# Reordering the layer steps of a six-layer kernel: projections first in a step, scores last, other PSUM banks

## The chip, the cores and the metric

The kernel runs on one core of one Trainium2 chip. The metric is the device time of one execution in microseconds (us). Below, PE is TensorE (matrix products), DVE is VectorE, ACT is ScalarE, POOL is GpSimd, and SP is the engine that issues most of the DMAs.

## The reference

The input x is 2048 tokens of 128 features. It is normalised to xn, and the result is the sum of three terms:

```
x = L0_attn_x                                   # 1 x 2048 x 128
xn = layernorm(x)
out = x + attention(xn) + layers(xn)

attention: 16 heads of 8, full softmax over 2048 keys, projections of rank 32
layers, 6 times:
  x = attn_layer(shift_tokens(x), Wqkv[i], q_scale[i], k_scale[i], Wo[i]) + x
  x = ffn_layer(shift_tokens(x), ln_g[i], ln_b[i], W1[i], b1[i], W2[i], b2[i]) + x

attn_layer: qkv = x @ Wqkv (128 x 3072); 16 heads of 64; q and k are divided by
  their norms, scaled, rotated; windows of 32 queries see their own and the
  previous window's keys; softmax; @ Wo (1024 x 128)
ffn_layer: layer norm, @ W1 (128 x 682), a * gelu(gate), @ W2 (341 x 128)
```

All is in float32. The kernel cuts the large products into two parts per operand (three products each) where it wants speed at float32 accuracy.

## The kernel before, in words

The program has two parts. Part A (until 780 us of the span) computes the full attention; the change does not touch it. Part B computes the six layers and adds the three terms.

Part B is a software pipeline that is written out by hand. The 2048 tokens of a layer are 16 tiles of 128, and 4 chunks of 512. Over six layers there are 96 tiles (END) and 24 chunks. Each of the five engines walks the same loop, `for u in range(FIRST, LAST)`, and in its step u calls its stages in a fixed order, each for the tile u minus an offset. Engines run in order, so a stage that waits holds up all that stand behind it on its engine. `tile(x)` is x if there is such a tile, `chunk(x)` is a chunk for one x in four (x = 4c + 3), `early(x)` is x for the first 4 steps, and `late(x)` is a chunk of the last layer.

The stages of a tile, in order of the data: `high_x` (ACT) and `low_x` (POOL) cut the input; `project` (PE, q, k, v, six products each); `squares` (ACT), `square_sums` and `root_argument` (DVE), `root_estimate` (ACT, three small operations), `root_slope` and `root_fix` (POOL): the norms; `rotate_cos`, `rotate_sin` (DVE, they read q or k in PSUM), `rotated`, `normalise` (POOL); `turn` (PE, transposes of q and k), `turned_q`, `turned_k` (ACT); `score` (PE, 128 small products), `maxima` (DVE), `exponentials` (ACT, 16 instructions), `prob_sums`, `prob_reciprocals` (DVE), `scale_probs` (POOL), `blocks` (DVE, a transpose within blocks), `move_probs` (SP, eight DMAs); `values` (PE, 128 small products), `values_out` (ACT), `output` (PE), `residual_1` (DVE). The stages of a chunk: `mean`, `deviation`, `deviation_squares`, `variance`, `add_epsilon`, `ln_root_estimate`, `first_scale`, `ln_root_slope`, `ln_root_fix`, `high_ln`, `scale_shift`, `low_ln`, `up_product` (three groups, 0, 2, 1), `gelu` (ACT, between two table loads), `gated` (DVE), `down_product`, `residual_2`.

Let v be the tile whose projection PE does in a step. Then v modulo 4 tells what else PE does in it: 0 variance and down product, 1 nothing, 2 the up products, 3 the mean.

PSUM has eight banks. The dictionary `BANKS` gives each stage its banks for even and odd units, `bank_users` walks PE's order, and `wait_free` makes a stage wait until the last user of each of its banks was read out.

The first four steps also finish part A's result ("dense" stages): `load_dense` (SP), `dense_norm` (DVE, a reciprocal and a product), `dense_output` on PE (L1396) and on ACT (L846), `store_dense` (SP). The last steps add up the result: `final_sum`, `finish`, `final_add`, `store_out`.

Of the kernel before, what the change touches and what calls it, by code (L numbers as in the profile page):

```python
# [16 lines left out]
NT = T // P  # L17
# [11 lines left out]
DEPTH = 6  # L29
# [37 lines left out]
FIRST, LAST = 0, END + 17  # L67
# [45 lines left out]
def late(x):  # L113
# [6 lines left out]
         "q_turn0": ((4,), (4,)), "q_turn1": ((1,), (5,)), "k_turn0": ((6,), (6,)),  # L120
         "k_turn1": ((0,), (7,)), "values": ((6, 7), (6, 7)), "output": ((7,), (7,)),
         "score": ((0, 1), (0, 1)), "mean": ((7,), (7,)), "var": ((4,), (4,)),
         "up0": ((4, 5), (4, 5)), "up1": ((2, 3), (2, 3)), "up2": ((6, 7), (6, 7)),
         "down": ((6,), (6,)), "att": ((7,), (5,)), "finish": ((7,), (7,))}
# [6 lines left out]
def bank_users():  # L131
# [9 lines left out]
    for u in range(FIRST, LAST):  # L141
        take("score", tile(u - 3))
        take("finish", late(u - 12))
        take("q", tile(u - 1))
        take("values", tile(u - 5))
        take("k", tile(u - 1))
        take("output", tile(u - 5))
        take("k_turn0", tile(u - 2))
        take("q_turn0", tile(u - 2))
        take("q_turn1", tile(u - 2))  # L150
        take("mean", chunk(u - 5))
        take("k_turn1", tile(u - 2))
        take("v", tile(u - 1))
        take("up0", chunk(u - 8))
        take("up2", chunk(u - 8))
        take("var", chunk(u - 6))
        take("down", chunk(u - 10))
        take("att", early(u))
        take("up1", chunk(u - 8))
# [250 lines left out]
def sync_b(e, w, m, s, d, out_rows):  # L410
# [93 lines left out]
    for x in range(min(0, -1), END + 12):  # L504
        if 0 < x < END:
            load_rot(x)
        n, i = divmod(x - 0, NT)
        if 0 < n < DEPTH and i == 0:
            load_qkv(n, 0)
        if tile(x - 3) is not None:  # L510
            shift_v(x - 3)
        if early(x - -1) is not None:
            load_dense(x - -1)
# [10 lines left out]
        if c is not None:  # L524
            store_out(c)
        n, i = divmod(x - 0, NT)
        if 0 < n < DEPTH and i == 0:
            load_qkv(n, 1)
        n, i = divmod(x - 7, NT)
        if 0 < n < DEPTH and i == 0:  # L530
            load_w1(n)
# [6 lines left out]
        if early(x - 0) is not None:  # L538
            store_dense(x - 0)
        if tile(x - 3) is not None:  # L540
            move_probs(x - 3)
        n, i = divmod(x, NT)
# [43 lines left out]
def gpsimd_b(e, w, m, s):  # L586
# [66 lines left out]
    for u in range(FIRST, LAST):  # L653
        low_x(tile(u))
        scale_probs(tile(u - 3))
        rotary(tile(u))
        rotated(tile(u - 1), 1)
        root_slope(tile(u - 1))
        root_fix(tile(u - 1))
        normalise(tile(u - 1), 1)  # L660
        normalise(tile(u - 1), 0)
        rotated(tile(u), 0)
# [39 lines left out]
def scalar_b(e, w, m, s):  # L702
# [147 lines left out]
    for u in range(FIRST, LAST):  # L850
# [638 lines left out]
```

## Time and profile before

| | |
|---|---|
| median of 3 runs | 2413.96 us |
| lowest, highest | 2406.57, 2416.26 us |
| profiled execution, its own time | 2408.15 us |
| its span in the profile | 2406.4 us |
| PE busy, share of the span | 90% |
| DVE busy | 83% |
| ACT busy | 73% |
| POOL busy | 54% |

The profiled execution is the source of every duration here. The profile's times count from the start of its span. "Busy" of PE is a modelled figure, since its products overlap.

### The profile page before, as it was taken

What the parts mean: (1) busy time and instruction counts of PE and PEld (TensorE: products, weight loads), DVE (VectorE), ACT (ScalarE), POOL (GpSimd) and SP (SyncE); (2) the same over time, 40 slices, a digit from 0 to 9 for tenths busy, and PEclk for the clock granted to TensorE, in tenths of its full rate; (3) what the DMA queues carried; (4) which work ended last, traced back from release to release, by engine and by line L of the source; (5) the groups of instructions that cost most, each with busy time, mean ns of one, the idle gap of its engine ahead of it and who ended that gap; (6) DMA issues with size and microseconds to landing.
All of it is one profiled execution on the core that took longest, in us unless ns stands there. A gap on an engine that the chain in (4) does not pass through costs nothing. (4 is left out here: it accounts for less than half of the span.)

```text
span 2406.4 us, 82195 instructions
## 1 busy us (share of the span) xinstructions
PE 2162.4 (90%) x34487; PEld 1324.6 (55%) x34487; DVE 2003.7 (83%) x2417; ACT 1758.8 (73%) x4192; POOL 1304.7 (54%) x1085
## 2 busy tenths in 40 slices
PE   5899999999998478989999999999998999999986
PEld 3122222222221267777777777777776777777764
DVE  6899999989992578878888888888988889898863
ACT  1187878878787267877888887788887778788762
POOL 4111111111000378877787887778887778787740
PEclk8599999999999789999999999999999999999987
DMA  1222322232201223343334333433334333433331
GB/s 35 72 75 68 88 55 82 63 83 54 52 22 67 83 68 85 80 123 86 91 82 129 89 89 82 117 101 94 84 84 115 89 92 86 123 92 97 87 80 40
DMA packets 167463, 197.60 MB, mean 82 GB/s; under 512 B 87479, under 2 KB 105141, under 8 KB 167093
## 3 DMA queue, kind: packets, MB, share of 16 engines
q1 hardware_dynamic: 166740, 192.14, 30.6%
q8 instruction: 271, 4.44, 0.8%
q14 instruction: 100, 0.81, 0.1%
q10 hardware_dynamic: 352, 0.20, 0.1%
HBM read 57.83 MB, written 27.26 MB: 35 GB/s over the span
## 5 line engine op out<-in xcount | busy, mean ns | idle before, releaser
L699 ACT ACTIVATE PT<-E_ps 128x512 f32<-128x512 f32 x1024 | 534.4, 601 | 182.3 <-PE E_ps L1242 180.6
L938 DVE TENSOR_REDUCE mx<-S_ps 128x1 f32<-128x1024 f32 x512 | 600.8, 1217 | 27.4 <-PE S_ps L1233 21.6
L639 POOL TENSOR_TENSOR tc<-tc,ts 128x1024 f32<-128x1024 f32 x192 | 462.5, 2409 | 53.8 <-DVE ts L1012 53.4
L647 POOL TENSOR_TENSOR tc<-tc,rs 128x1024 f32<-128x1024 f32 x192 | 362.3, 1909 | 13.8
L1233 PE MATMUL S_ps<-KS,QS 48*128 48x512 bf16 x1024 | 324.9, 401 | 30.4 <-DVE mx L938 22.0
L581 POOL CAST w_cut_b<-w_raw_b 128x512 fp32r<-128x512 f32 (+1 forms) x48 | 27.6, 576 | 550.4 <-DMA w_raw_b<-in_Wqkv 409.8
L762 ACT ACTIVATE pr<-B_ps,mxB 128x64 f32<-128x64 f32 x1536 | 325.0, 372 | 0.0
L1242 PE MATMUL E_ps<-QS,KS 64*128 64x512 bf16 x1024 | 316.2, 385 | 4.7 <-ACT PT L699 4.6
L601 POOL TENSOR_TENSOR pr<-pr,mxB 128x1024 f32<-128x1024 f32 x96 | 184.0, 1916 | 193.5 <-DVE mxB L1045 193.5
L1000 DVE TENSOR_TENSOR tc<-B_ps,rt 128x1024 f32<-128x1024 f32 x192 | 234.8, 1223 | 49.9 <-ACT nrm L710 44.4
L1250 PE MATMUL O_ps<-PT,va 128*32 128x512 f32 x2048 | 276.0, 611 | 0.0
L1274 PE MATMUL B_ps<-w_qkv,x_cut 128*128 128x512 f32 x576 | 262.8, 456 | 10.5 <-ACT q_T L732 6.4
L1242 PEld LDWEIGHTS E_ps<-QS,KS 64*128 64x128 bf16 x1024 | 78.5, 94 | 317.5 <-ACT PT L699 236.3
L710 ACT ACTIVATE nrm<-B_ps 128x1024 f32<-128x1024 f32 x192 | 208.4, 1085 | 61.2 <-PE B_ps L1276 59.0
L1275 PE MATMUL B_ps<-w_qkv,x_cut 128*128 128x512 f32 x576 | 233.5, 405 | 1.9 <-issue 1.9
L1276 PE MATMUL B_ps<-w_qkv,x_cut 128*128 128x512 f32 x576 | 233.3, 405 | 2.1 <-issue 2.1
L982 DVE TENSOR_REDUCE ss<-nrm 128x16 f32<-128x1024 f32 x192 | 232.0, 1208 | 0.0
L1337 PE MATMUL B_ps<-xy,vs 64*64 64x32 f32 x6144 | 204.2, 222 | 23.9 <-issue 16.2
L1337 PE MATMUL B_ps<-xy,v 64*64 64x32 f32 x6144 | 204.4, 222 | 21.3 <-issue 20.8
L1337 PEld LDWEIGHTS B_ps<-xy,vs 64*64 64x64 f32 x6144 | 181.4, 137 | 61.4 <-issue 60.7
L752 ACT ACTIVATE o_T<-B_ps 128x1024 f32<-128x1024 f32 x96 | 98.7, 1028 | 156.7 <-PE B_ps L1337 156.7
L1300 PE MATMUL B_ps<-ident,tc 128*128 128x128 f32 x1536 | 198.6, 276 | 15.6 <-DVE ts L1012 8.9
(191 smaller groups left out, 4139.8 us busy)
## 6 DMA issues: line engine op xcount, KB each, us to landing
xy<-pc SPq DMA_DIRECT2D x768, 64.0 KB, 2.4
vs<-v SPq DMA_DIRECT2D x96, 384.0 KB, 3.7
Wqkv_cut<-w_cut_b SPq DMA_DIRECT2D x72, 256.0 KB, 2.4
w_qkv<-Wqkv_cut SPq DMA_DIRECT2D x36, 512.0 KB, 7.3
rot<-in_rot SPq DMA_DIRECT2D x96, 128.0 KB, 2.7
vs<-v SPq DMA_DIRECT2D x96, 128.0 KB, 3.7
w_raw_b<-in_Wqkv SPq DMA_DIRECT2D x36, 256.0 KB, 3.1
W_cut<-w_cut_b SPq DMA_DIRECT2D x24, 170.5 KB, 2.5
```

The source lines that it names most:

```text
L639: e.tensor_tensor(tc[:, :], tc[:, :], m.ts[i][:, :], ALU.add).then_inc(s[f"rot{n}"], 1)
L647: e.tensor_tensor(tc, tc, m.rs[u % 2][2][:, i * H:(i + 1) * H].unsqueeze(2).to_broadcast([P, H, DH]), ALU.mult).then_inc(s[f"{n}_scaled"], 1)
L699: e.activation(m.PT[n % NPT][:, :], turns.bank("probs", n)[:, :], ACT.Exp).then_inc(turns.sem("probs", n), 1)
L762: a = e.activation(pb[:, :, h, :], sc[:, h, :, :], ACT.Exp, bias=m.mxB[:, 0, h:h + 1], scale=1.0)
L938: e.tensor_reduce(m.mx[h % 2][:, i, hf:hf + 1], m.S_ps[n % 2][:, :, :], AX.XY, ALU.max).then_inc(s["sc_max"], 1)
L1000: e.tensor_tensor(view(m.tcs[u % 2][i][:, :]), raw, wide(m.rt[u % 2][:, 2 * i, :], DH), ALU.mult).then_inc(s[f"rot{n}_c"], 1)
L1233: mm = e.matmul(m.S_ps[n % 2][:, c, :], m.QS[sl][rows, i * P:(i + 1) * P], m.KS[sl][rows, k:k + CH], start=True, stop=True)
L1242: e.matmul(turns.bank("probs", n)[:, :], m.KS[sl][rows, j * P:(j + 1) * P], m.QS[sl][rows, chunk_cols(c)], start=True, stop=True).then_inc ...
L1250: e.matmul(m.O_ps[VC * c:VC * (c + 1), :], m.va[:, j, h, :], m.PT[n % NPT][:, :], start=(j == 0), stop=(j == NT - 1)).then_inc(s["pv"], 1)
L1274: e.matmul(bank, left[0], right[0], start=True, stop=False)
L1275: e.matmul(bank, left[0], right[1], start=False, stop=False)
L1337: mm = e.matmul(bank[at, a, j, b, :], v[r, d:d + DH], m.xy[u % 2][r, b, par * NP + j, :], start=(b == j == 0), stop=True, skip_group_check ...
```

## The change

Each engine's order of stages within a step is changed, and with it the offsets, so that a step starts with `project` and ends with `score`. LAST is END + 16 in place of END + 17. `BANKS` changes for five stages. SP's order changes in four places. No instruction is added or removed, and no size changes.

```diff
-FIRST, LAST = 0, END + 17
+FIRST, LAST = 0, END + 16
...
-         "q_turn0": ((4,), (4,)), "q_turn1": ((1,), (5,)), "k_turn0": ((6,), (6,)),
+         "q_turn0": ((4,), (4,)), "q_turn1": ((6,), (5,)), "k_turn0": ((1,), (6,)),
...
-         "score": ((0, 1), (0, 1)), "mean": ((7,), (7,)), "var": ((4,), (4,)),
+         "score": ((0, 1), (0, 1)), "mean": ((6,), (6,)), "var": ((4,), (4,)),
...
-         "down": ((6,), (6,)), "att": ((7,), (5,)), "finish": ((7,), (7,))}
+         "down": ((5,), (5,)), "att": ((4,), (7,)), "finish": ((7,), (7,))}
```

PE, in tensor_b (bank_users has the same order):

```diff
-        score(tile(u - 3))
-        finish(late(u - 12))
-        project(tile(u - 1), 0)
-        values(tile(u - 5))
-        project(tile(u - 1), 1)
-        output(tile(u - 5))
-        turn(tile(u - 2), 1, 0)
-        turn(tile(u - 2), 0, 0)
-        turn(tile(u - 2), 0, 1)
-        mean(chunk(u - 5))
-        turn(tile(u - 2), 1, 1)
-        project(tile(u - 1), 2)
-        up_product(chunk(u - 8), 0)
-        up_product(chunk(u - 8), 2)
-        variance(chunk(u - 6))
-        down_product(chunk(u - 10))
-        dense_output(early(u))
-        up_product(chunk(u - 8), 1)
+        finish(late(u - 11))
+        project(tile(u), 0)
+        values(tile(u - 4))
+        project(tile(u), 1)
+        output(tile(u - 4))
+        turn(tile(u - 1), 0, 0)
+        turn(tile(u - 1), 0, 1)
+        turn(tile(u - 1), 1, 0)
+        turn(tile(u - 1), 1, 1)
+        project(tile(u), 2)
+        up_product(chunk(u - 7), 0)
+        up_product(chunk(u - 7), 2)
+        up_product(chunk(u - 7), 1)
+        variance(chunk(u - 5))
+        dense_output(early(u))
+        mean(chunk(u - 4))
+        down_product(chunk(u - 9))
+        score(tile(u - 1))
```

DVE, in vector_b:

```diff
-        gated(chunk(u - 9), 2)
-        final_sum(late(u - 11))
-        ln_root_slope(chunk(u - 7))
-        maxima(tile(u - 3))
-        rotate_cos(tile(u - 1), 0)
-        square_sums(tile(u - 1), 0)
-        rotate_sin(tile(u - 1), 0)
-        ln_root_fix(chunk(u - 7))
-        residual_1(tile(u - 5))
-        prob_sums(tile(u - 3))
-        low_ln(chunk(u - 8))
-        rotate_cos(tile(u - 1), 1)
-        prob_reciprocals(tile(u - 3))
-        rotate_sin(tile(u - 1), 1)
-        dense_norm(early(u))
-        final_add(late(u - 11))
-        square_sums(tile(u - 1), 1)
-        root_argument(tile(u - 1))
-        gated(chunk(u - 8), 0)
-        gated(chunk(u - 8), 1)
-        deviation(chunk(u - 5))
-        add_epsilon(chunk(u - 6))
-        blocks(tile(u - 3))
-        residual_2(chunk(u - 10))
-        first_scale(chunk(u - 6))
+        low_ln(chunk(u - 7))
+        first_scale(chunk(u - 6))
+        maxima(tile(u - 2))
+        rotate_cos(tile(u), 0)
+        ln_root_fix(chunk(u - 6))
+        rotate_sin(tile(u), 0)
+        square_sums(tile(u), 0)
+        residual_1(tile(u - 4))
+        prob_sums(tile(u - 2))
+        dense_norm(early(u))
+        prob_reciprocals(tile(u - 2))
+        rotate_cos(tile(u), 1)
+        rotate_sin(tile(u), 1)
+        add_epsilon(chunk(u - 5))
+        final_add(late(u - 10))
+        square_sums(tile(u), 1)
+        deviation(chunk(u - 4))
+        gated(chunk(u - 7), 0)
+        gated(chunk(u - 7), 1)
+        residual_2(chunk(u - 9))
+        blocks(tile(u - 2))
+        final_sum(late(u - 9))
+        root_argument(tile(u))
+        gated(chunk(u - 7), 2)
+        ln_root_slope(chunk(u - 5))
```

ACT, in scalar_b:

```diff
+        scale_shift(chunk(u - 9))
+        root_estimate(tile(u - 3))
+        squares(tile(u - 2), 0)
+        values_out(tile(u - 6))
         exponentials(tile(u - 4))
+        turned_q(tile(u - 3), 0)
         squares(tile(u - 2), 1)
-        turned_q(tile(u - 3), 0)
         turned_q(tile(u - 3), 1)
+        dense_output(early(u - 2))
+        turned_k(tile(u - 3), 1)
         turned_k(tile(u - 3), 0)
-        turned_k(tile(u - 3), 1)
         keep_v(tile(u - 2))
-        deviation_squares(chunk(u - 6))
-        high_ln(chunk(u - 8))
         ln_root_estimate(chunk(u - 7))
-        dense_output(early(u - 1))
         gelu_table(chunk(u - 9))
         gelu(chunk(u - 9), 0)
-        high_x(tile(u))
+        high_ln(chunk(u - 8))
         gelu(chunk(u - 9), 1)
         gelu(chunk(u - 9), 2)
         root_table(chunk(u - 9))
-        scale_shift(chunk(u - 8))
-        root_estimate(tile(u - 2))
-        squares(tile(u - 1), 0)
-        values_out(tile(u - 5))
+        high_x(tile(u))
+        deviation_squares(chunk(u - 6))
```

POOL, in gpsimd_b:

```diff
-        low_x(tile(u))
-        scale_probs(tile(u - 3))
-        rotary(tile(u))
-        rotated(tile(u - 1), 1)
-        root_slope(tile(u - 1))
-        root_fix(tile(u - 1))
-        normalise(tile(u - 1), 1)
-        normalise(tile(u - 1), 0)
-        rotated(tile(u), 0)
+        rotated(tile(u - 2), 1)
+        rotary(tile(u - 1))
+        root_slope(tile(u - 2))
+        root_fix(tile(u - 2))
+        normalise(tile(u - 2), 0)
+        normalise(tile(u - 2), 1)
+        rotated(tile(u - 1), 0)
+        low_x(tile(u))
+        scale_probs(tile(u - 3))
```

SP, in sync_b:

```diff
         if 0 < x < END:
             load_rot(x)
-        n, i = divmod(x - 0, NT)
-        if 0 < n < DEPTH and i == 0:
-            load_qkv(n, 0)
         if tile(x - 3) is not None:
             shift_v(x - 3)
-        if early(x - -1) is not None:
-            load_dense(x - -1)
...
+        n, i = divmod(x - 7, NT)
+        if 0 < n < DEPTH and i == 0:
+            load_w1(n)
         n, i = divmod(x - 0, NT)
         if 0 < n < DEPTH and i == 0:
             load_qkv(n, 1)
-        n, i = divmod(x - 7, NT)
-        if 0 < n < DEPTH and i == 0:
-            load_w1(n)
...
-        if early(x - 0) is not None:
-            store_dense(x - 0)
+        if early(x - 1) is not None:
+            store_dense(x - 1)
         if tile(x - 3) is not None:
             move_probs(x - 3)
+        if early(x - -1) is not None:
+            load_dense(x - -1)
+        n, i = divmod(x - -1, NT)
+        if 0 < n < DEPTH and i == 0:
+            load_qkv(n, 0)
```

## Rows read from the trace of the kernel before

**Rows 1.** Busy time by window: us, then PE, PEld, DVE, ACT, POOL, PEclk, DMA.

```profile
780.00:869.00 89.00, 43.22 (x519) 29.75 (x520) 54.16 (x54) 32.63 (x84) 40.88 (x37) 0.73 0.26 73
869.00:2363.00 1494.00, 1389.46 (x29591) 1100.10 (x29592) 1260.34 (x1652) 1168.89 (x3052) 1152.23 (x926) 0.98 0.37 94
```

**Rows 2.** PE's waits from 780 us on: us in total, times, longest.

```profile
PE B_ps L1337 <- issue: 37.1, 39, 3.3
PE B_ps L1396 <- DVE hid L1153: 27.1, 2, 23.6
PE B_ps L1320 <- issue: 14.9, 8, 5.2
PE B_ps L1315 <- ACT k_T L744: 9.3, 23, 0.4
PE B_ps L1274 <- ACT q_T L732: 6.4, 21, 0.3
PE B_ps L1274 <- DMA w_qkv<-Wqkv_cut: 1.6, 2, 1.0
```

**Rows 3.** Timeline of PE, first steps of part B: start, us, instruction, idle before.

```profile
799.36 2.08 PE L1396 MATMUL B_ps<-hid,w_out 128*128 128x512 f32 x2 [23.62 <-DVE hid L1153]
...
818.10 0.76 PE L1274 MATMUL B_ps<-w_qkv,x_cut 128*128 128x512 f32 x1 [0.87 <-ACT xl L846]
...
834.07 1.06 PE L1315 MATMUL B_ps<-mask_bf,ident_bf 128*128 128x512 bf16 x2
...
836.53 0.50 PE L1274 MATMUL B_ps<-w_qkv,x_cut 128*128 128x512 f32 x1
...
868.74 0.50 PE L1274 MATMUL B_ps<-w_qkv,x_cut 128*128 128x512 f32 x1
```

**Rows 4.** Timelines of POOL, DVE and ACT in the same stretch.

```profile
781.31 0.46 POOL L594 TENSOR_TENSOR x_cut<-stream,x_cut 128x128 fp32r<-128x128 f32 x1
795.23 3.35 DVE L1151 RECIPROCAL hid<-hid 128x512 f32<-128x512 f32 x1 [12.15 <-DMA hid<-l_scratch]
798.62 0.69 DVE L1153 TENSOR_TENSOR hid<-hid 128x512 f32<-128x512 f32 x1
801.48 0.69 ACT L846 ACTIVATE hid<-B_ps,bo 128x512 f32<-128x512 f32 x1 [20.53 <-PE B_ps L1396]
```

**Rows 5.** Timelines of ACT and PE, a step with v = 1 modulo 4.

```profile
1519.15 1.03 ACT L752 ACTIVATE o_T<-B_ps 128x1024 f32<-128x1024 f32 x1 [2.69 <-PE B_ps L1337]
1523.22 1.15 ACT L710 ACTIVATE nrm<-B_ps 128x1024 f32<-128x1024 f32 x1
1526.98 0.59 PE L1315 MATMUL B_ps<-mask_bf,ident_bf 128*128 128x512 bf16 x2 [0.40 <-ACT k_T L744]
```

**Rows 6.** Timelines of DVE and PE, end of a step with v = 2 modulo 4.

```profile
2048.05 0.28 DVE L990 TENSOR_SCALAR rs<-ss 128x32 f32<-128x32 f32 x1
2050.27 1.23 DVE L1023 STREAM_TRANSPOSE pc<-pr 128x1024 f32<-128x1024 f32 x1
2051.43 0.70 DVE L1111 SCALAR_TENSOR_TENSOR hid<-B_ps,b,gel 85x512 f32<-85x512 f32 x1
2052.28 0.32 PE L1337 MATMUL B_ps<-xy,vs 64*64 64x32 f32 x8
```

**Rows 7.** Timelines of DVE and PE, end of a step with v = 0 modulo 4.

```profile
1509.67 1.21 DVE L982 TENSOR_REDUCE ss<-nrm 128x16 f32<-128x1024 f32 x1
1511.15 0.68 DVE L1073 TENSOR_SCALAR lnv<-B_ps 128x512 f32<-128x512 f32 x1
1513.63 0.76 DVE L1125 SCALAR_TENSOR_TENSOR stream<-B_ps,cols,stream 64x512 f32<-64x512 f32 x1
1508.71 2.74 PE L1388 MATMUL B_ps<-hid,w 128*128 128x512 f32 x6
1513.22 0.50 PE L1274 MATMUL B_ps<-w_qkv,x_cut 128*128 128x512 f32 x1
```

**Rows 8.** Timeline of PE in the last steps.

```profile
2355.81 0.50 PE L1274 MATMUL B_ps<-xl_cut,w 128*128 128x512 f32 x1 [1.41 <-DVE xl_cut L1103]
```

More of the change, by code:

```diff
@@ L141, in bank_users @@
     for u in range(FIRST, LAST):
[L142 to L157, printed above, removed]
+        take("finish", late(u - 11))
+        take("q", tile(u))
+        take("values", tile(u - 4))
+        take("k", tile(u))
+        take("output", tile(u - 4))
+        take("q_turn0", tile(u - 1))
+        take("q_turn1", tile(u - 1))
+        take("k_turn0", tile(u - 1))
+        take("k_turn1", tile(u - 1))
+        take("v", tile(u))
+        take("up0", chunk(u - 7))
+        take("up2", chunk(u - 7))
+        take("up1", chunk(u - 7))
+        take("var", chunk(u - 5))
         take("att", early(u))
-        take("up1", chunk(u - 8))
+        take("mean", chunk(u - 4))
+        take("down", chunk(u - 9))
+        take("score", tile(u - 1))
     return users
```

## The prediction

> **What bounds the kernel now.** I read the busy times by window first. From 869 to 2363 us PE is busy for 1389 of 1494 us, at a mean granted clock of 0.98 of full speed; DVE has 84% and ACT 78%. In the 89 us ahead of that, PE is busy for under half, and the clock is 0.73 [rows 1]. So the steady part of part B is bound by PE with some waits, and its start by something else. Then I read PE's waits [rows 2]. "Issue" (PE waits for nothing the profile shows) inside the two runs of 128 small products, values and scores, is 52.0 us: 37.1 + 14.9. Waits for ACT (k_T, q_T) are 15.7 us, in steps with v = 1 and 3 modulo 4. One wait of 23.6 us stands alone: PE's first instruction of part B is the dense product, and it waits for DVE. Last come the timelines of those places.
>
> **The offsets.** Each engine's order is a circle, and what counts is which stages follow each other and for which tile. PE before, in step u = v + 1: scores of tile v - 2, project v, values v - 4, turns v - 1, up v - 7, down v - 9. After, in step u = v: the same tiles, with scores of v - 1 at the end, which is scores of v - 2 ahead of the next. So in the steady state PE's circle is the old one but for small swaps: turns q, q, k, k; the mean behind the v projection; the third up group is already next to the others, as variance and down fall into other steps. ACT's and POOL's circles are also the old ones with neighbours swapped. "One stage less" is therefore no shorter pipeline for a tile; only the dense stages, tied to early(u), move against the rest. The total of the work is the same, and I look for places where a swap touches the path.
>
> **Start of part B (the large term).** Before, PE's step 0 holds only the dense product. It needs a load, then 3.35 and 0.69 us of DVE, and starts at 799.36 [rows 3, 4]. The first projection, whose cut input was ready at 781.31 + 0.46 = 781.8 [rows 4], stands behind it, and the second tile's starts at 818.10 [rows 3]. After, the first tile is projected at 781.8 and the dense product comes behind it. Its data decide as before: I keep 799.4, + 2.08, + 0.69 on ACT (q of the second tile now shares its bank 4) = 802.2 for the second tile's q. That is 818.1 - 802.2 = 15.9 us earlier. Next step, from 802.2: six products at 1.2 GHz, 2.6 (512 columns, 0.43 each); squares 1.1; cosine 1.2 (as the sums), sine in two halves of 0.6, sums 1.2; the dense reciprocal and product 4.0, the dense product on PE 2.1 and its read-out 0.7, which now stands ahead of turned_k on ACT, 1.5; scores 2.5 (834.07 to 836.53). With 0.1 for hand-overs the sum is 18.2, so the third tile's q starts at 820.4, against 836.53 before: 16.1 earlier [rows 3 to 5, 7]. Two steps follow. Before they took 868.74 - 836.53 = 32.2 us, since the last dense product was done early in them [rows 3]. After, both hold one; with a warm PE and the exponentials (3.1 us, 1520.2 to 1523.2 [rows 5]) beside the same list I get 17.0 + 16.7 = 33.7. Bounds: 32.2 as before, and 2 x 18.4 = 36.8 as the step 818.1 to 836.5. The steady state starts 14.6 us earlier (bounds 16.1 and 11.5; at the cheap end nothing is lost again, at the dear end both steps are full ones). The cover of this: nothing in the steady state can give it back, as the whole pipeline starts earlier and PE is its bound.
>
> **Steps with v = 1 and 3 (neutral).** After the values product ACT reads it out (1519.15), does 16 exponentials, then squares of k (1523.22), two q and four k read-outs, and the scores start at 1526.98, having waited 0.40 [rows 5]. The change swaps squares with the first q read-out and the two k's; the list until the last k is the same. The q that the v projection waited for comes 0.95 us earlier, so those 6.4 us of waits go, and the scores' wait for k_T grows by as much: the scores' start is late next, and it is unmoved. The mean behind v instead of ahead of it changes nothing in the sum of PE work ahead of the scores. Gain 0; bounds -6.4 (if ACT's chain had slack) and +2 (24 steps of v = 1 with 0.1 of a swap).
>
> **Steps with v = 2 (a small loss).** The banks 6 and 7 that up group 2 used are the values product's next, so values waits for gated 2. The row shows gated 2 from 2051.43 to 2052.13 and values 0.15 us behind it, at 2052.28 [rows 6]; in all 22 such steps that I read, values starts 0.14 to 0.16 us behind the end of gated 2. This is the path. On it stand gelu 1, gated 1, blocks and gated 2. The change puts root_argument between blocks and gated 2; it occupies DVE for 0.18 us (the 0.28 at 2048.05 overlaps its successor [rows 6]). 23 steps x 0.18 = +4.1 us. Gated 1 can't be earlier, since it waits for the last up product, so the removal of root_argument (and of low_ln, 0.7) ahead of it gives nothing. Bounds 0 and +6.4 (0.28 each).
>
> **Steps with v = 0 (neutral, tight).** The down product moves from bank 6 to 5. Its reader residual_2 now holds up the next q projection (banks 4, 5), 1.6 us sooner than the values product it held up before. Down ends at 1508.71 + 2.74 = 1511.45. DVE, done with the sine at 1509.67, has epsilon 0.60 and sums 1.13 (each less than its row by what overlaps), so it is free at 1511.40, then residual_2, 1.48 for its two halves: 1512.97, + 0.14 = 1513.1. The projection starts at 1513.22 [rows 7]. Slack 0.1: no cost. Bounds 0 and 24 x 0.3 = +7. Blocks and root_argument come 1.5 us behind their old place there; root_estimate then ends about 2 us into the next step, and POOL's fix and two scalings (4.7 us) end at 6.9, where the q turns start and the k turns are 0.9 later. Q is scaled first now, so this holds too.
>
> **SP.** The weights of the next layer's q are issued ahead of load_rot, not behind. One issue is 0.6 us, and the projection waited for that load for 1.6 us in all [rows 2]: -1.6. Load_rot is later by 1.2 to 2 us once a layer; rotary, also one place later on POOL, covers it. The eight moves behind blocks start up to 1.5 us later in one step of four; the values product that needs them is over a step away.
>
> **End.** The last-but-one up product waited 1.41 us for low_ln, which stood behind residual_1 [rows 8]. Now it stands at the head of the step: -1.4. The last chunk's chain is the same.
>
> Sum: -14.6 + 4.1 - 1.6 - 1.4 = -13.5 us. The profiled execution took 2408.15 us (span 2406.4 and 1.75 around it), so 2394.7 for the same execution. The median of the runs shown is 2413.96, 5.8 above it, and I put the difference on the median: 2400.5 us.
>
> The Trainium skill, "Runtime: NRT & Kernel Launch", section "Instruction fetch mechanics", says that an engine fetches its instructions in blocks of 256 while it executes, and that this is hidden. The 52 us of issue in dense runs [rows 2] do not agree if they are fetches. By the page they would be no fetches and the new order would leave them alone, which is my sum; if they are fetches, it may move them, which bears on the first rival's chance.
>
> **Rivals.** (1) Slower: the moves. The eight DMAs behind blocks start 1.5 us later in the 24 steps with v = 0, and so lie wholly over the next values run, the place of most issue waits. For it: those waits are of no engine, so something outside, such as DMA traffic, makes them. Against it: they overlapped that run in part already, and the waits also stand in other steps. Mean of one wait is 37.1 / 39 = 0.95, longest 3.3 [rows 2]; I take 1.5 with what it does to the clock: 24 x 1.5 = +36, so 2436. It decides the sign from 0.56 us a step. (2) The start gains little: rt, loads or the read-out that now stands ahead of turned_k stretch each of the first steps by 2 to 3 us, so that 5 of 14.6 us are left: 2410. For it: DVE is in every one of these steps with 4 us of dense work. Against it: each link was there before. (3) More: bundled waits ahead of the scores give the issue side time, and a third to a half of the 52 us goes: -20, so 2380. For it: the scores' wait becomes one of about 0.9 us just ahead of a dense run. Against it: steps that had such a wait have issue waits as well.
>
> **How the numbers follow.** Forecast 0.55 (its own range 2394 to 2408); rival 1 0.12; rival 2 0.18; rival 3 0.15. About 0.5% (12.1 us) is what a measurement of this kernel can tell from no change. Faster than 2401.9: 0.38 of the forecast, 0.15, and 0.02 of rival 2: 0.55. Within: 0.17 + 0.16 + 0.02 = 0.35. Slower: 0.10. The range reaches from near rival 3 to between rivals 2 and 1: 2383 to 2418.
>
> **What would show it.** Right: PE's first projection at 782; second tile's q at about 802, fifth's at 854 (868.74 before); values still 0.15 us behind gated 2, with L990 between it and blocks; waits for q_T gone and those for k_T doubled; issue waits within a few us of 52. Wrong: a fifth projection after 860 (rival 2), issue waits over 75 us or under 35 us (rivals 1, 3), or q projections that wait for residual_2 (DVE stream, L1125).

## The result, and the profile after

The changed kernel takes 2425.07 us (median; 2417.14 to 2440.6), the kernel before 2414.29 beside it: a ratio of 1.0052 [1.0036, 1.0068] (95% interval), or 12.5 us slower (10.8 between the medians). Once more on another chip it was 1.0036 [1.0013, 1.0059]. The forecast was 2400.5 us and faster; it was wrong in sign, and the range ended at 2418, below both medians (2425.07 and 2420.8).

The profiled execution has a span of 2422.3 us (own time 2424.12) against 2406.4. Busy time by window, the columns as in [rows 1]; the second window goes from the first values product of part B to the last:

```profile
780.00:869.00 89.00, 50.93 (x532) 32.58 (x535) 56.70 (x54) 38.28 (x93) 41.49 (x36) 0.79 0.27 75
872.00:2377.00 1505.00, 1382.23 (x29556) 1097.78 (x29555) 1271.91 (x1650) 1166.65 (x3052) 1151.58 (x922) 0.98 0.36 94
```

PE does the same work at the same clock in 1505 us that took it 1492: the time is idle time. PE's waits from 780 us on show which, answering [rows 2]:

```profile
PE B_ps L1320 <- issue: 35.1, 21, 4.1
PE B_ps L1337 <- issue: 32.4, 41, 3.6
PE B_ps L1315 <- ACT k_T L744: 24.6, 25, 2.3
PE B_ps L1396 <- DVE hid L1153: 14.1, 2, 11.3
```

The waits for q_T are gone, those for k_T have grown (between 869 and 2378 us from 9.3 to 20.0), the wait for w_qkv is gone (1.6 before; 0.2 in a second profile of the changed kernel). What is new is "issue" inside the scores (L1320): 8 waits and 14.9 us have become 21 and 35.1. In values and scores together, the 52.0 us of the prediction have become 67.5. Over all lines of the steady part (from the first values product to the last) the issue waits are 53 with 57.4 us before and 69 with 74.7 us after.

The start, PE's timeline with the answers to [rows 3]: dense product, projections of q for tiles 0 to 4:

```profile
793.07 0.77 PE L1274 MATMUL B_ps<-w_qkv,x_cut 128*128 128x512 f32 x1 [6.12 <-ACT x_cut L782]
...
810.62 2.07 PE L1396 MATMUL B_ps<-hid,w_out 128*128 128x512 f32 x2 [11.31 <-DVE hid L1153]
813.56 0.76 PE L1274 MATMUL B_ps<-w_qkv,x_cut 128*128 128x512 f32 x1 [0.87 <-ACT hid L846]
...
828.84 0.59 PE L1315 MATMUL B_ps<-mask_bf,ident_bf 128*128 128x512 bf16 x2 [2.31 <-ACT k_T L744]
830.78 0.50 PE L1274 MATMUL B_ps<-w_qkv,x_cut 128*128 128x512 f32 x1
...
851.03 0.80 PE L1274 MATMUL B_ps<-w_qkv,x_cut 128*128 128x512 f32 x1
...
869.64 0.79 PE L1274 MATMUL B_ps<-w_qkv,x_cut 128*128 128x512 f32 x1
```

Part A, whose code is the same in both, ends where ACT cuts the first tile (L782): at 791.84 here, at 780.63 before. I count from there, since the end of part A lies anywhere between 774.7 and 791.8 in the profiles of this study. The second tile's q stood 37.5 us behind it and now stands 21.7, as forecast; the fifth's 88.1 and 77.8.

Split of four executions, from the timelines (us; "start" is from the end of part A to the first values product, "values" from the first to the last of the 96):

| | end of part A | start | values | rest | span |
|---|---|---|---|---|---|
| before | 780.6 | 89.7 | 1492.2 | 43.8 | 2406.4 |
| changed | 791.8 | 80.5 | 1504.7 | 45.3 | 2422.3 |
| changed, again (e8) | 785.1 | 81.5 | 1504.7 | 45.3 | 2416.6 |
| best (e14) | 783.1 | 69.5 | 1463.9 | 43.7 | 2360.2 |

So the change gains 8 to 9 us at the start and loses 12.5 us in the steady part, the same in two executions, and 1.5 at the end.

What an issue wait is can be read at one of the longest, in the scores of a step with v = 3 modulo 4. PE's timeline:

```profile
1049.88 1.07 PE L1300 MATMUL B_ps<-ident,tc 128*128 128x128 f32 x8 [0.22 <-ACT pr L762]
...
1053.16 0.60 PE L1315 MATMUL B_ps<-mask_bf,ident_bf 128*128 128x512 bf16 x2
1053.70 1.37 PE L1320 MATMUL B_ps<-k_T,q_T 64*32 64x64 f32 x115
1059.21 0.34 PE L1320 MATMUL B_ps<-k_T,q_T 64*32 64x64 f32 x13 [4.15 <-issue]
```

PE stands with 13 of 128 products to go, and nothing it needs is late. The DMA view of the window 1056.70 to 1056.95 has a row (packets, MB, share) that the windows around it, 1050 to 1056.7 and 1056.95 to 1059.2, do not have:

```profile
q8 instruction: 1, 0.02, 26.9%
```

That queue brings PE's instructions: 271 fetches of 16 KB in an execution, for 69,596 recorded instructions of PE, so 257 to a fetch. The steady part has 234 of them. This one began at 1056.85, and ended 1.3 us before the products went on. The same holds for all 53 waits before and all 69 after, and for 739 of 747 issue waits in fifteen profiles of this study: the last fetch began 2.2 to 3.0 us before the wait's end and ended 1.2 to 1.75 us before it. (In e3, the sixteenth, about a third of 87 waits have no such fetch.) The scores are about 260 instructions in 1.9 us and values 256 in 2.0 us (a matmul comes with its weight load), so a run of them is shorter than the 2.2 us from a fetch's start to the wait's end. If a fetch starts only inside or just ahead of such a run, PE can run out of instructions.

Before and after have almost the same PE stream (69,505 and 69,596 recorded instructions), with the same dense runs. What differs is the waits. A matmul (in the trace, its weight load) carries one wait itself; each further wait goes into separate instructions ahead of it. There are 529 such before and 620 after, so the change does add instructions, 91 waits on PE, though it adds no work: 48 more because k_turn0 of an even tile now lies in bank 1, where the previous scores were, and so waits for the exponentials (smexp) besides k_scaled; 23 ahead of the mean, 21 ahead of projections, and one less elsewhere. In the profile after, fetches start while PE is in the turns 0 times instead of 6, and in the scores 17 times instead of 8, in steps with v = 3.

Theory L: a separate wait that is not yet satisfied holds PE's sequencer, which otherwise runs ahead of PE and asks for the next instructions early. Rivals: R (the new orders on ACT and DVE are late on the path), B (the banks: who waits for whom), N (the number of instructions and where the blocks fall).

### The profile page after: what moved, and what is told of

Same layout as the page of the kernel before. It is cut to its first block and busy times, and to the rows that moved or that the text cites. A ratio compares the mean times of both kernels' runs of the same rounds, so it can differ in the third digit from the quotient of the medians.

```text
span 2422.3 us, 82286 instructions
## 1 busy us (share of the span) xinstructions
PE 2171.9 (90%) x34487; PEld 1328.2 (55%) x34487; DVE 2018.9 (83%) x2417; ACT 1756.9 (73%) x4192; POOL 1306.8 (54%) x1085
## 5 line engine op out<-in xcount | busy, mean ns | idle before, releaser
L938 DVE TENSOR_REDUCE mx<-S_ps 128x1 f32<-128x1024 f32 x512 | 601.3, 1217 | 36.9 <-PE S_ps L1233 31.2
L639 POOL TENSOR_TENSOR tc<-tc,ts 128x1024 f32<-128x1024 f32 x192 | 456.3, 2377 | 101.4 <-DVE ts L1012 101.3
L647 POOL TENSOR_TENSOR tc<-tc,rs 128x1024 f32<-128x1024 f32 x192 | 371.3, 1955 | 13.8
L1233 PE MATMUL S_ps<-KS,QS 48*128 48x512 bf16 x1024 | 330.7, 408 | 31.2 <-DVE mx L938 22.0
L1242 PE MATMUL E_ps<-QS,KS 64*128 64x512 bf16 x1024 | 321.6, 391 | 4.6 <-ACT PT L699 4.6
L1250 PE MATMUL O_ps<-PT,va 128*32 128x512 f32 x2048 | 282.9, 625 | 0.0
L1349 PEld LDWEIGHTS B_ps<-o_T,w_o 128*128 128x128 f32 x1536 | 191.4, 196 | 15.8 <-ACT o_T L752 6.8
```

What stands on the lines that cost most here:

```text
L639: e.tensor_tensor(tc[:, :], tc[:, :], m.ts[i][:, :], ALU.add).then_inc(s[f"rot{n}"], 1)
L647: e.tensor_tensor(tc, tc, m.rs[u % 2][2][:, i * H:(i + 1) * H].unsqueeze(2).to_broadcast([P, H, DH]), ALU.mult).then_inc(s[f"{n}_scaled"], 1)
L938: e.tensor_reduce(m.mx[h % 2][:, i, hf:hf + 1], m.S_ps[n % 2][:, :, :], AX.XY, ALU.max).then_inc(s["sc_max"], 1)
L1233: mm = e.matmul(m.S_ps[n % 2][:, c, :], m.QS[sl][rows, i * P:(i + 1) * P], m.KS[sl][rows, k:k + CH], start=True, stop=True)
L1242: e.matmul(turns.bank("probs", n)[:, :], m.KS[sl][rows, j * P:(j + 1) * P], m.QS[sl][rows, chunk_cols(c)], start=True, stop=True).then_inc ...
L1250: e.matmul(m.O_ps[VC * c:VC * (c + 1), :], m.va[:, j, h, :], m.PT[n % NPT][:, :], start=(j == 0), stop=(j == NT - 1)).then_inc(s["pv"], 1)
```

## Experiments

All ratios are against the kernel before, run beside each kernel. "Start" and "values" are as in the split above, from one execution each. "Issue" is the sum of issue waits in the steady part (before: 57.4 us in 53; changed: 74.7 in 69).

| kernel | ratio [95%] | start | values | issue |
|---|---|---|---|---|
| e1 start alone | 1.0028 [1.0004, 1.0052] | 95.4 | 1495.6 | 55.0 |
| e2 banks as before | 0.9907 [0.9874, 0.9940] | 80.2 | 1483.7 | 51.7 |
| e3 root_argument early | 1.0362 [1.0328, 1.0396] | 80.6 | 1590.1 | 84.2 |
| e4 ACT's order | 1.0049 [1.0021, 1.0077] | 81.5 | 1513.8 | 77.9 |
| e5 e2 + unsatisfied waits | 1.0046 [1.0026, 1.0066] | 80.7 | 1514.9 | 77.3 |
| e6 e2 + satisfied waits | 0.9913 [0.9885, 0.9940] | 78.8 | 1482.7 | 55.8 |
| e7 late wait attached | 0.9867 [0.9845, 0.9889] | 80.2 | 1469.7 | 46.5 |
| e8 changed again | 1.0036 [1.0013, 1.0059] | 81.5 | 1504.7 | 74.3 |
| e9 e7, read-out late | 0.9806 [0.9770, 0.9842] | 69.8 | 1472.8 | 43.9 |
| e10 two waits swapped | 0.9895 [0.9859, 0.9931] | 82.8 | 1473.0 | 52.7 |
| e11 carrier | 0.9807 [0.9774, 0.9840] | 80.1 | 1459.0 | 36.9 |
| e12 before, late attached | 0.9867 [0.9831, 0.9903] | 91.1 | 1472.6 | 39.5 |
| e13 start with DVE's line | 0.9966 [0.9945, 0.9987] | 81.2 | 1503.1 | 62.4 |
| e14 best | 0.9776 [0.9738, 0.9813] | 69.5 | 1463.9 | 39.8 |

**e1.**

```
-        dense_output(early(u))        # PE
+        dense_output(early(u - 1))    # behind the projections of its tile
-        dense_norm(early(u))          # DVE, same place
+        dense_norm(early(u - 1))
...                                   # and ACT's read-out, SP's loads and stores, banks 4 and 7
```

> The kernel before with the start of part B alone changed: the dense product stands behind the projections of its step on PE, its reciprocal and product one step later on DVE, its read-out behind the second q read-out on ACT, its loads and stores moved on SP as in the change, banks 4 and 7. Steady state as before. Theory L (the loss lies in the steady state, in PE's instruction fetches): the start gains what it gained in the change, 9 us from the end of part A to the first values product, and nothing is lost behind it: 9 to 15 us faster, about 2403, issue waits about 57 us in part B. Rival S (the start gives nothing that lasts, or costs it back): within 4 us of the time before, about 2412.

A miss on the start: it costs 5.7 us instead of gaining, and the kernel is 0.28% slower. The steady part is nearly that of before (+3.4). So neither theory: see e13.

**e2.**

```
-         "q_turn0": ((4,), (4,)), "q_turn1": ((6,), (5,)), "k_turn0": ((1,), (6,)),
+         "q_turn0": ((4,), (4,)), "q_turn1": ((1,), (5,)), "k_turn0": ((6,), (6,)),
-         ... "mean": ((6,), (6,)) ...
+         ... "mean": ((7,), (7,)) ...
```

> The changed kernel with three bank shares as before: second q turn in bank 1, first k turn in 6, mean in 7; all orders stay. This takes away 48 separate wait instructions on PE (the wait for the exponentials ahead of the k turns goes onto the second q turn, which has no other) and 23 ahead of the mean. Theory L: with these waits gone PE's sequencer runs ahead again, the instruction fetches start sooner, and issue waits of part B fall from 75 us to about 60; 12 to 18 us faster than the changed kernel, so 2408 to 2413, 0 to 6 us faster than before. Rival R (the orders of ACT and DVE cost it): issue waits stay at 75 us and the time at 2425, 12 us slower than before.

Three bank numbers turn 0.5% slower into 0.9% faster, more than L forecast. The waits in the scores are back to what they were; PE's waits:

```profile
PE B_ps L1337 <- issue: 30.1, 29, 3.3
PE B_ps L1300 <- ACT pr L762: 23.2, 42, 0.6
PE B_ps L1315 <- ACT k_T L744: 21.9, 25, 2.5
PE B_ps L1320 <- issue: 13.1, 8, 3.1
```

The wait for the exponentials is now a plain one of 0.55 us on the second q turn (23.2 us in 42), dearer by itself than the 7.5 us in 32 of the changed kernel, and still the kernel is faster. All orders stay as changed, so R is out as the main cause; B is not yet.

**e3.**

```
         square_sums(tile(u), 1)
+        root_argument(tile(u))
...
         blocks(tile(u - 2))
         final_sum(late(u - 9))
-        root_argument(tile(u))
```

> The changed kernel with root_argument right behind the second square sums on DVE, as before. Rival R, its DVE part (root_estimate waits 76 times, 105 us in sum, for the late root_argument, and with it ACT's whole list): 8 to 16 us faster than the changed kernel, 2409 to 2417. Theory L: only the 0.18 us ahead of gated 2 in 23 steps comes back, 4 us: 2421, and issue waits stay at about 75 us.

Both theories miss it by 80 us: 3.6% slower. The groups of DVE from 872 to 2377 us (instructions | busy us, mean ns of one) name it; first e3, then the changed kernel:

```profile
L990 DVE TENSOR_SCALAR rs<-ss 128x32 f32<-128x32 f32 x89 | 108.1, 1215 | 8.6 <-issue 0.4
```

```profile
L990 DVE TENSOR_SCALAR rs<-ss 128x32 f32<-128x32 f32 x92 | 26.8, 291 | 0.0
```

The same instruction takes 1215 ns instead of 291. DVE and POOL in e3, one step:

```profile
1510.97 1.39 DVE L990 TENSOR_SCALAR rs<-ss 128x32 f32<-128x32 f32 x1
...
1509.93 2.40 POOL L639 TENSOR_TENSOR tc<-tc,ts 128x1024 f32<-128x1024 f32 x1 [0.82 <-DVE ts L1012]
```

It ends with POOL's product, at 1512.36 and 1512.33. Of the 96 in e3, 95 began inside that POOL instruction, and each ended 0.03 to 0.05 us behind its end. So this small operation of DVE is held until POOL's product is done. Not every operation is: DVE's reductions of probabilities took 1.22 us both inside such a product and outside it. In the kernel before it stood at the same place in DVE's list and took 0.28 us, since in 85 of 96 cases POOL's order had another instruction there (L614); in the changed kernel it starts near the end of POOL's product (28 of 96) or outside it. The Trainium skill, "GPSIMD Engine Reference", section "1. Specifications", says that the SBUF interfaces are shared with VectorE and contend for some DVE instructions; the trace agrees, with 1215 ns against 291. The new place of root_argument goes with the new order on POOL: undone alone, it costs 85 us of the steady part.

**e4.**

```
+        squares(tile(u - 2), 1)
         turned_q(tile(u - 3), 0)
-        squares(tile(u - 2), 1)
         turned_q(tile(u - 3), 1)
         dense_output(early(u - 2))
-        turned_k(tile(u - 3), 1)
         turned_k(tile(u - 3), 0)
+        turned_k(tile(u - 3), 1)
```

> The changed kernel with ACT's order of before between the exponentials and keep_v: squares of k ahead of the q read-outs, k read-outs 0 then 1. Rival R, its ACT part (the swap makes the scores' wait for k_T grow from 9.3 to 24.6 us): 6 to 12 us faster than the changed kernel, 2413 to 2419. Theory L: the k read-outs end at the same time either way; within 3 us of the changed kernel, 2425, issue waits about 75 us, the wait for k_T about 25 us.

As L says: no gain, with issue at 77.9 us. The wait for k_T fell to 18.3 us, but that for q_T came back with 9.6. The swap moves waits between two names, as I had forecast; ACT's order is not the cause. (Its profiled steady part, 1513.8 us, is 9 us longer than the changed kernel's, while the medians differ by 1 us: such a part of a single execution is not exact to a few us.)

**e5 and e6.** Both are e2 with one redundant wait on the second q turn of even tiles. Same banks, same dependencies, 597 separate waits in both.

```
         w.wait_ge(s["k_scaled" if i else "q_scaled"], u + 1)
+        if name == "q_turn1" and u % 2 == 0:      # e5: smexp goes into the separate wait
+            e.wait_ge(s["q_scaled"], u + 1)
         banks.wait_free(w, name, u)
+        if name == "q_turn1" and u % 2 == 0:      # e6: a satisfied one goes there
+            e.wait_ge(s["idb"], 1)
```

> The kernel of e2 (banks 1, 6 and 7 as before) with one redundant wait more in the steps that turn an even tile: q_turn1 waits for q_scaled again (long satisfied, it rides on the transposition), which pushes its wait for the exponentials into a separate wait instruction in front, 48 in all. The dependencies are those of e2. Theory L (a separate wait that is not yet satisfied holds PE's sequencer, so that the next instruction fetch starts late): most of the gain of e2 goes, issue waits rise from 52 to about 70 us, time 2408 to 2425. Rival B (it was the banks, that is who waits for whom): as e2, 2393, issue waits about 52.

> The kernel of e2 with the same 48 separate wait instructions as e5 in the same places, but they are for a semaphore that was set at the start of the program, and the wait for the exponentials stays on the transposition. As long a stream as e5's and the same 256-instruction blocks. Theory L: a satisfied wait holds nothing, so as e2: 2393 within 4 us, issue waits about 52. Rival N (the number of instructions or where the blocks fall decides): as e5, 10 to 30 us slower than e2.

e5 loses all that e2 gained, e6 nothing. The issue waits in values (L1339) and scores (L1322), e5 then e6:

```profile
PE B_ps L1339 <- issue: 37.5, 40, 3.6
PE B_ps L1322 <- issue: 31.4, 18, 4.5
```

```profile
PE B_ps L1339 <- issue: 32.7, 38, 3.2
...
PE B_ps L1322 <- issue: 13.5, 9, 4.3
```

B is out, as the banks are the same, and N, as the number is. 48 unsatisfied separate waits cost 32 us from first to last values product: 21.5 us are issue waits, and 10.0 us are a longer busy time of PE, whose clock was at the lower of its two levels for 75.1 us in e5 and 61.4 in e6. That is what theory L says. Its inner link, that a held sequencer asks for the next block late, is read from where the fetches start; no run moves a fetch and nothing else. Of the fetches in steps with v = 1 and 3, e6 starts 10 while PE is in the turns and 24 in the scores, e5 starts 2 and 32. The Trainium skill, "Perfetto Trace Analysis", section "Sequencer Loop", says that engine instructions are pushed into a queue and wait there for semaphores, while control instructions are executed by the sequencer. e5 against e6 agrees, with 1.0046 and 0.9913.

**e10.** The changed kernel with two lines swapped:

```
-        w.wait_ge(s["k_scaled" if i else "q_scaled"], u + 1)
         banks.wait_free(w, name, u)
+        w.wait_ge(s["k_scaled" if i else "q_scaled"], u + 1)
```

> The changed kernel with nothing but two waits ahead of the turns swapped in the text: the bank's reader is named first and so rides on the transposition, and the scaling is in the separate wait. Same banks, same orders, same number of separate waits (619). Ahead of the k turns of even tiles PE's sequencer then waits for the scaling of k (0.9 us behind that of q) and no more for the exponentials. Theory L: most of the loss goes: 10 to 22 us faster than the changed kernel, 2400 to 2412, issue waits of part B 55 to 65 us. Rivals B and N (banks, or the number of instructions): 2423 within 4 us.

The first wait named is the one that rides on the matmul: in the trace, 47 separate instructions that wait for smexp are gone, and 47 weight loads of the turns carry it instead. (The swap also puts q_scaled into the separate wait ahead of the q turns; the result is net of that.) With smexp there and k_scaled in the separate wait, the changed kernel gains 1.4%: banks, orders and number of waits are untouched. Its median was 2386.04 beside 2412.39 for before. Again more than forecast (2400 to 2412).

```profile
PE B_ps L1315 <- ACT k_T L744: 37.2, 48, 2.7
PE B_ps L1337 <- issue: 35.6, 38, 3.3
...
PE B_ps L1320 <- issue: 10.3, 7, 3.6
```

The issue waits in the scores fall from 35.1 to 10.3 us. The wait for k_T grows by 12.6 and takes part of this back.

**e7.** e2, and the late wait named first elsewhere too:

```
 # project, values: banks.wait_free(...) moved to the front; score:
-        w.wait_ge(s["qT_out0"], u + 1)
-        w.wait_ge(s["qT_out1"], u + 1)
+        if u % 2:
+            w.wait_ge(s["v_out"], min(u + 2, END))
         w.wait_ge(s["kT_out0"], u + 1)
-        w.wait_ge(s["kT_out1"], u + 1)
         w.wait_ge(s["mask"], 1)
-        banks.wait_free(w, "score", u)
```

> The kernel of e2 with the latest wait of a stage on the matmul itself and the early ones in the separate instruction: projections and values name the bank's reader first, and the scores wait only for the last of ACT's read-outs (v's where v shares the bank, else the first half of k_T), which come in ACT's order. Separate waits that are unsatisfied when PE's sequencer reaches them: those ahead of the scores in the odd half of the steps and ahead of the q projection go. Theory L: issue waits fall from 52 to 25 to 40 us, 2370 to 2385, a new best. Rival B: the end of a wait is where it was, so nothing changes, 2393 within 4 us.

Time as L forecast; the issue waits fell a little less (46.5). Those in the scores are all but gone (4 with 4.8 us). Values follows gated 2 faster as well: 0.05 to 0.06 us behind its end in all 23 steps, against 0.14 to 0.15 in both kernels of this case. Worked out from that, up to 5 of the 32 us between e5 and e6 (48 waits of 0.1 us, an estimate) may be a later release and no fetch. e12 puts the same placing on the kernel before:

> The kernel before with only the placing of waits as in e7 (bank's reader first in projections and values, the scores behind ACT's last read-out alone); no order and no bank changed. Theory L: it takes issue waits out of the kernel before as well, from 57 to about 40 us: 8 to 15 us faster, 2399 to 2406. If waits placed so help only with the changed orders: within 3 us of before.

(Its edit is that of e7, but with kT_out1, which is ACT's last there, for kT_out0, and with values naming its two bank readers in the other order.) It gains 1.3% (32 us), more than forecast, with no engine's order changed, so the placing of waits is worth something without the change too. And e7, with the new orders and the same kind of placing, has the same ratio, 0.9867: between these two, the new orders bring nothing clear of noise.

**e8.** The changed kernel, unedited.

> The changed kernel once more, on the same chip as e5 to e7: 0.3 to 0.7% slower than the kernel before. Its second profile shows how much of one execution's split is chance: part A (the same code in both) ended 11 us later in the first profile of the changed kernel, with a clock of 0.97 against 0.99; I expect its end between 780 and 792, and the steady part 11 to 14 us longer than before again (theory L), with 65 to 80 us of issue waits in part B. A rival that the loss is part A's says: the steady part is then within 4 us of before.

The steady part took 1504.7 us again. Part A ended at 785.1, so its 791.8 in the first profile was chance in good part.

**e11.** e7 with the changed kernel's turn banks; smexp on the fourth transposition of the second q turn, where nothing else waits:

```
-        for had, n in self.m.users[stage, unit]:
+        for had, n in self.m.users[stage, unit][::-1 if stage == "values" else 1]:
...
         for j in range(4):
+            if name == "q_turn1" and j == 3 and u % 2 == 0:
+                banks.wait_free(w, "k_turn0", u)
             b = 4 * hf + j
```

> The kernel of e7 with the changed kernel's banks for the turns (second q turn in 6, first k turn in 1), and the wait for the exponentials attached to the fourth transposition of the second q turn, where nothing else waits; values names the later of its two bank readers first. The dependencies of the changed kernel are there, without its separate wait. Theory L: at least as fast as e7, since the second q turn no longer stands wholly behind the exponentials (PE waited 23.5 us for them in e7, 7.5 to 9.2 in the changed kernel): 2370 to 2381. Rival B: these banks cost 20 us or more: 2400 or above.

0.9807, below the forecast's lower end (2366.4 us). The turn banks of the change cost nothing here; where their wait stood was bad. How much of the gain over e7 is theirs, and how much the new order of the two waits ahead of values, these runs do not separate.

**e9.** e7, with one line of ACT moved:

```
-        dense_output(early(u - 2))
         turned_k(tile(u - 3), 1)
         turned_k(tile(u - 3), 0)
         keep_v(tile(u - 2))
+        dense_output(early(u - 2))
```

> The kernel of e7 with ACT's read-out of the dense product behind keep_v instead of ahead of the k read-outs. This is my step for the start of part B: I put that read-out on the path of the first four tiles, and they took 80 us from the end of part A to the first values product (89.7 before, 75.1 forecast). If it is what ate the rest, the scores of tiles 1 to 3 start 1.3 to 2.3 us sooner behind the dense product (3.4 to 4.4 us after its start in the changed kernel), the first values product comes 74 to 77 us behind the end of part A, and the time is 3 to 6 us less than e7's 2381. Rival: the dense product itself, behind DVE's list, sets these steps; then within 2 us of e7, and 79 to 81 us to the first values product.

The start shrinks from 80.2 to 69.8 us, more than I had sized, and the time by about 15 us (0.9867 to 0.9806) where I had 3 to 6. PE in the second step, e7 and then e9:

```profile
820.38 1.12 PE L1394 MATMUL B_ps<-gel,w_out 128*128 128x512 f32 x2
...
823.78 0.60 PE L1313 MATMUL B_ps<-mask_bf,ident_bf 128*128 128x512 bf16 x2 [2.27 <-ACT k_T L744]
```

```profile
808.34 1.13 PE L1394 MATMUL B_ps<-gel,w_out 128*128 128x512 f32 x2 [0.32 <-DVE gel L1153]
809.52 0.38 PE L1313 MATMUL B_ps<-mask_bf,ident_bf 128*128 128x512 bf16 x1
```

With the read-out ahead of the k read-outs the scores wait 2.3 us behind the dense product; with it behind, they follow at once.

**e13.** e1 with one line of DVE moved:

```
+        dense_norm(early(u - 1))
         rotate_cos(tile(u - 1), 1)
         prob_reciprocals(tile(u - 3))
         rotate_sin(tile(u - 1), 1)
-        dense_norm(early(u - 1))
```

> The kernel of e1 (the kernel before with only the start of part B changed) with one line of DVE moved as in the change: the dense product's reciprocal and product stand ahead of prob_reciprocals and the second cosine, not behind the second sine. If that place made e1 slower (from the end of part A to its first values product it took 95.4 us; before 89.7, changed 80.5 and 81.5), it now takes 79 to 84 us, and the time is 6 to 12 us less than before, about 2403. Rival (ACT's and POOL's orders of the change made its start, not DVE's): 92 us or more, and a time as e1's, 0 to 0.5% more than before.

It holds: 81.2 us, and 0.34% faster than before, with 8.5 us of the start and 10 us in the time. DVE's reciprocal in the second step of e1 and e13 (end of part A 783.25 and 783.42):

```profile
816.36 3.34 DVE L1151 RECIPROCAL gel<-gel 128x512 f32<-128x512 f32 x1
```

```profile
812.19 3.34 DVE L1151 RECIPROCAL gel<-gel 128x512 f32<-128x512 f32 x1
```

In e1 it stands behind the cosine and sine of k, and with it the dense product, the read-outs and the scores are late in each of the first four steps. The values part of e13 was 1503.1 us, 11 more than before: 5 us more issue, and 6.7 us more busy time of PE, whose clock was at the lower level for 92.2 us of it, against 68.3 before. What brought the clock down more often is open.

**e14.** e11 with the lines of e9 and e10.

> The kernel of e11 (changed orders and turn banks, exponentials' wait on the fourth transposition, late waits on the matmul) with ACT's read-out of the dense product behind keep_v as in e9, and the bank's reader first at the turns as in e10. The gains are in different places: 80.1 to about 70 us from the end of part A to the first values product (e9: 69.8), values to values 1459 us (e11: 1459.0). Against before: 0.9807 and a start worth another 0.4%: 0.974 to 0.979, 2350 to 2362. Rival (the start's gain is given back, as before it was given back in the steady part): as e11, 0.981.

0.9776, the fastest kernel of the study. The start keeps its gain (69.5 us); the steady part, 1463.9, is 5 us longer than e11's. The interval still reaches the rival's 0.981; the start in the profile speaks against it.

## Why the prediction was wrong

**The step that failed** is "issue waits within a few us of 52" (values and scores), and behind it "PE's circle is the old one but for small swaps". I held that the new order leaves those waits alone, and wrote them into the sum as zero. In values and scores they grew from 52.0 to 67.5 us, over all lines of the steady part by 17.3 us, and 48 waits that were placed badly cost about 32 us (e5 against e6). With these waits moved onto the matmul, and nothing else undone, the changed kernel is 1.0 to 1.1% faster than before (e10, 0.9895), so the sign of my sum hangs on this step. The other terms do not make up for it: in the profiles, the start is 5.9 us short of its forecast, the steady part 10.0 us over it (12.5 for 2.5), the end 2.9 over. That turns -13.5 into +5.3. I had the rows to doubt it: [rows 2] show waits that no engine causes, and I wrote what it would mean if they were fetches. What I did not look at is on which instruction each wait sits, and that a bank adds a wait: "No instruction is added or removed" held for the work alone. The Trainium skill, "Runtime: NRT & Kernel Launch", section "Instruction fetch mechanics", calls the crossing of a block mostly hidden; here 53 and 69 of the 234 fetches of the steady part were not, and the measurement decides.

**Rival 1** had the sign, but not its mark or its mechanism. The mark was 75 us where before had 52.0; the same lines now have 67.5 (all lines of the steady part: 74.7). Later moves over the values run would have made the waits in values grow; those fell (37.1 to 32.4), and the scores', where no move was added, more than doubled. e6 has the moves of the changed kernel and loses nothing.

**The start** was mis-sized: 8 to 9 us instead of 14.6. The first steps came as forecast, the second tile's q 21.7 us behind part A (15.8 sooner, forecast 15.9). The third tile's is 17.2 behind it (forecast 18.2). The fourth and fifth are 20.3 and 18.6 apart, where I took 17.0 and 16.7, and 18.4 as the dear end. The read-out ahead of turned_k, which I sized at 0.7 us of ACT, leaves PE waiting 2.3, 3.3 and 2.3 us ahead of the scores in these steps. Behind the second of these waits the projections run at 1.2 GHz (0.63 us each; 0.39 us before, at 2.4 GHz). With the read-out moved the start is 10.4 us shorter (e9). And the gain is not a property of the dense stages' offset: with that alone the start is 5.7 us longer (e1), with DVE's place of dense_norm 8.5 shorter (e13). Rival 2 described this (it names "the read-out that now stands ahead of turned_k") but gave it 9.6 us where 5 to 6 were lost, and its mark, a fifth projection after 860, was not reached: counted from the end of part A of before, it came at 858.4 (forecast 854).

**Steps with v = 1 and 3**: q_T's waits went and k_T's doubled, as forecast (6.4 to 0; 9.3 to 20.0), and e4 shows by its time that this is neutral. The steps became longer all the same, by the issue waits. **Steps with v = 2**: the mechanism was right. Timelines of DVE and PE after, answering [rows 6]:

```profile
2065.13 1.24 DVE L1023 STREAM_TRANSPOSE pc<-pr 128x1024 f32<-128x1024 f32 x1
2066.29 0.14 DVE L990 TENSOR_SCALAR rs<-ss 128x32 f32<-128x32 f32 x1
2066.34 0.74 DVE L1111 SCALAR_TENSOR_TENSOR hid<-B_ps,b,gel 85x512 f32<-85x512 f32 x1
...
2067.23 0.32 PE L1337 MATMUL B_ps<-xy,vs 64*64 64x32 f32 x8
```

Values is still 0.15 us behind gated 2 in all 23 steps, with L990 in between; the median step, from values to values, grew by 0.11 us (16.75 to 16.86), so this term is 2 to 3 us, not 4.1. **Steps with v = 0**: no projection waits for residual_2, as forecast; the median step still grew from 15.89 to 15.97 and 16.09 in the two profiles. **SP**: right in both profiles (1.6 to nothing and to 0.2), but e10, with the same order of SP, has 3.1 us of this wait. **End**: the wait of 1.41 us went, but the rest took 1.5 us more, not 1.4 less, as the last up product waits longer for xl_cut (3.36 against 2.83) and the down product before it ran slower (4.28 against 3.79).

**What stays open.** From the end of part A on the changed kernel loses 4.8 and 5.8 us in its two profiles; the medians say 9 to 12.5. The rest would lie in part A, whose end varies by 17 us between profiles and follows the clock granted in it (0.952 of full speed where it ends at 774.7, 0.947 at 780.6, 0.928 at 791.8). These profiles can't settle whether the change has a part in that. Nor do I know what makes the sequencer ask for a block when it does: the fetch at 1056.85 came 1.8 us after PE had run dry.

## What to carry over

Where several waits stand ahead of a matmul, only the first named rides on it. Put the one that comes last there (e7, e10, e12), or give it to an instruction of the stage before that has no other (e11); an unsatisfied wait in a separate instruction was what cost time (e5), a satisfied one was free (e6). Two lines swapped for that were worth more here than the whole reordering (about 36 us against 12.5). Idle time that the profile gives to "issue" in dense runs of small matmuls is a term of its own: look at the instruction queue's fetches just ahead of it, and count which waits a reordering or a bank adds.

## What I had not expected of the hardware

- PE stood for 37 to 78 us of about 1500 behind instruction fetches (e11 and e4; fifteen profiles), nearly all of it in runs of some 256 small instructions that last 2 us, where a fetch and what follows it take 2.2 to 3.0 us.
- 48 separate waits cost 32 us if unsatisfied, and nothing if satisfied (1514.9 against 1482.7 us).
- One DVE operation (L990) on 128 x 32 elements takes 0.29 us, or up to the end of a POOL instruction of 2.4 us that runs beside it (1.2 us in the mean); 95 of these made the steady part of e3 85 us longer.
